# A graph-layer kernel on one core: adj as the weights of the last two row tiles, a bias spread by a matmul, weights on a block diagonal

## Chip, core and metric

One Trainium2 chip, one of its cores. The metric is the device time of one execution in microseconds (us); lower is better. Before the change it is 250.76 us, the median of 3 runs (250.6 to 250.86).

## What is computed

N = 5000 nodes, 64 features, all float32; `adj` is 5000 x 5000 and dense in memory (100 MB).

```python
h = jnp.maximum(_layernorm(x, axis=-1), 0.0)
neighbors = adj @ h
neighbors = neighbors / (num_neighbors[:, None] + 1e-7)
out = jnp.concatenate([h, neighbors], axis=-1) @ fc_w.T + fc_b
return x + jax.nn.relu(out)
```

The kernel multiplies first by the right half of `fc_w` (g = h @ W2.T) and then by `adj`, so that for every node out = x + relu(h @ W1.T + b + (adj @ g) / count).

## The kernel before

`adj` comes transposed, in three column groups of 2048, 2560 and 392 columns (GROUPS, WIDTH). Its 5000 rows are cut into 39 tiles of 128 (CH = 39), and 8 rows are left over (REM). A tile of `raw` holds 128 rows (the contraction) of a group's columns (output nodes). `multiply` (L574) has the 64 columns of g of that tile as stationary weights and streams the adj columns past them. The sums stand in the PSUM tensors acc0 to acc5 with features on the lanes; acc5 is the tensor `turned`, which takes the last 392 columns in two sides of SIDE = 196. A float32 matmul runs as two instructions, each with its own load of weights, so one tile of the last group is 4 instructions.

The order of TensorE's work is written out by hand: over all loads in order, with the steps of the layer norm's transposes (`turn`, TURN_AFTER), the weighing (`weigh`, WEIGH_AFTER), the counts (`spread`), the 8 remaining rows (`remainder`) and the turning back of finished banks (`flip`, FLIP_AFTER) put in after named tiles. A group's sums go back to node-major by `scale` (DVE, with the reciprocal count), `flip` (PE transpose) and `finish` (DVE, relu and x).

The last 392 columns end the kernel. `preload_self` (L611) puts the self part of the 392 nodes into y0 and y1 as the start of a sum. After tile 38, `scale_last` (L474) multiplies the sums by the reciprocal counts into sums0, `flip_last` (L618) adds their transpose to y0 and y1, `finish_last` (L491) applies relu and adds x, and SP stores 98 KB (L243) and waits for it. The 392 nodes stand on 98 lanes (LAST_LANES), four to a lane.

The SP queue issues x (L236, L239) and then all 40 adj loads (`load`, L224). A load waits on `load_used` when its place in `raw` is still in use. The ACT queue issues the two copies of the weights and the bias (`load_weights`, L278), the counts, the 8 remaining rows of each group (`load_rem`, L264) and the stores of the first two groups. The 8 rows stand on lanes 0, 4, ..., 28 of `adj_rem` (REM_STEP = 4); its other lanes are zero, and so are those of `ht_rem`.

`weigh` takes two node tiles at a time, in the lane halves of `ht`. Each half has its own matmul with the copy of the weights in the same half of `w_both`: 64 lanes by 128 columns, self and neighbour part. `copy_g` (ACT) takes the neighbour part and `add_bias` (DVE) the self part plus the bias.

Of the kernel before, what the change touches and what calls it, by code (L numbers as in the profile page):

```python
# [12 lines left out]
LANES = 128  # L13
# [8 lines left out]
REM_STEP = 4  # L22
# [17 lines left out]
def gnn_layer(nc, x, adj_groups, num_neighbors, fc_t, fc_b, out):  # L40
# [69 lines left out]
    PRELOAD_AFTER = (2, 25)  # L110
    LN_OPS = 8

    with ExitStack() as ctx:
# [22 lines left out]
        w_both = sb("w_both", [2 * F, 2 * F])  # L136
# [3 lines left out]
        ones = sb("ones", [LANES, HALF])  # L140
# [3 lines left out]
        rstd = sb("rstd", [LANES, BT])  # L144
        warm = sb("warm", [LANES, 1])
# [10 lines left out]
        nn_loaded = sem("nn_loaded")  # L156
        weights_loaded = sem("weights_loaded")
        bias_loaded = sem("bias_loaded")
        landed = [sem(f"landed{k}") for k in range(LANDINGS)]
# [15 lines left out]
        self_copied = sem("self_copied")  # L175
        spread_done = sem("spread_done")
# [6 lines left out]
        out_ready = sem("out_ready")  # L183
        stored = sem("stored")
# [29 lines left out]

        def bcast(v):
            return v.unsqueeze(2).to_broadcast([LANES, v.shape[1], F])
# [6 lines left out]
        @block.sync  # L223
        def _(sp):  # L224
            def load(n):
                g, m, i0, i1 = LOADS[n]
                w = WIDTH[g]
                if loads_before(n):
                    sp.wait_ge(load_used, loads_before(n))
                r = RUN if m < FULL else TAIL_RUN  # L230
                rows = adj_groups[g][m * BLOCK:m * BLOCK + r * LANES, 0:w].rearrange("(p i) c -> p (i c)", i=r)
                sp.dma_start(raw[:, place(n):place_end(n)], rows[:, i0 * w:i1 * w]).then_inc(loaded(n)[0], 16)  # L232

            for k in range(2):
# [12 lines left out]
        def _(pool):  # L247
# [3 lines left out]
                                    pattern=[[-1, LANES]], channel_multiplier=1).then_inc(ident_ready, 1)  # L251
            nc.gpsimd.memset(adj_rem[:], 0.0).then_inc(rem_cleared, 1)
            nc.gpsimd.memset(ones[:], 1.0).then_inc(ones_ready, 1)
# [3 lines left out]
            pool.wait_ge(ones_ready, 2)  # L257
# [5 lines left out]
        def _(act):  # L263
            def load_rem(g):  # L264
                w = WIDTH[g]
                if g:
                    act.wait_ge(rem_used, g)
                else:
                    act.wait_ge(rem_cleared, 2)
                lanes = slice(0, REM * REM_STEP, REM_STEP)  # L270
                k = w // BLOCK
                if k:
                    act.dma_start(adj_rem[lanes, 0:k, 0:BLOCK],
                                  adj_groups[g][REM0:N, 0:w].rearrange("r (k c) -> r k c", k=k)).then_inc(rem_loaded, 16)
                else:
                    act.dma_start(adj_rem[lanes, 0, 0:w], adj_groups[g][REM0:N, 0:w]).then_inc(rem_loaded, 16)

            def load_weights():  # L278
                for s in range(2):
                    act.dma_start(w_both[s * F:(s + 1) * F, :].rearrange("r (k c) -> r k c", k=2),  # L280
                                  fc_t.rearrange("(k r) c -> r k c", k=2)).then_inc(weights_loaded, 16)
                act.dma_start(bias[:], fc_b.rearrange("(a f) -> a f", a=1).to_broadcast([LANES, F])
                              ).then_inc(bias_loaded, 16)
# [32 lines left out]
            def copy_g(b):  # L316
                act.wait_ge(weighed, b + 1)
                for s in range(2):
                    t0 = BT * b + RUN * s
                    nc.scalar.activation(g_sb[:, t0:t0 + RUN, :], split(y[s][:])[:, :, F:2 * F], ACT.Copy  # L320
                                         ).then_inc(g_copied, 1)
# [14 lines left out]
            load_weights()  # L336
# [17 lines left out]
            store(1)  # L354
            act.wait_ge(stored, 32)

        @block.vector
        def _(dve):
            nc.vector.memset(warm[:], 1.0).then_inc(warm_ready, 1)
            nc.vector.memset(x_sb[PAD0:LANES, ROWS:TILES, :], 0.0).then_inc(x_cleared, 1)  # L360
            nc.vector.memset(nn[:], 1.0).then_inc(nn_cleared, 1)
# [11 lines left out]
            def normalize(b):  # L373
                base = LN_OPS * b
                dve.wait_ge(x_loaded[0], 32)
                if b == SETS - 1:
                    dve.wait_ge(x_loaded[1], 16)
# [26 lines left out]
            def add_bias(b):  # L404
                if b == 0:
                    dve.wait_ge(bias_loaded, 16)
                for s in range(2):
                    m = 2 * b + s
                    to = blocks(out_sb, m, m + 1) if m < FULL else out_sb[:, ROWS:TILES, :]
                    dve.wait_ge(g_copied, 2 * b + s + 1)  # L410
                    nc.vector.tensor_tensor(to, split(y[s][:])[:, :, 0:F],  # L411
                                            bias[:].unsqueeze(1).to_broadcast([LANES, RUN, F]),
                                            ALU.add).then_inc(self_copied, 1)
# [60 lines left out]
            def scale_last(g):  # L474
                wait_sums(g, LAST)
                dve.wait_ge(flipped, LAST)
                for i in range(2):
                    nc.vector.tensor_tensor(sums[0][:, i * LAST_LANES:(i + 1) * LAST_LANES],  # L478
                                            tile_major(acc[LAST][:, 0:SIDE], 2)[:, i, :],
                                            rnn_bc[:, ALONE, BLOCK // 2 + i * LAST_LANES:BLOCK // 2 + (i + 1) * LAST_LANES],  # L480
                                            ALU.mult).then_inc(scaled, 1)
# [9 lines left out]
            def finish_last():  # L491

                for i in range(2):
                    dve.wait_ge(flipped, LAST + i + 1)
                    done = nc.vector.scalar_tensor_tensor(  # L495
                        tail_half(out_sb, i), y[i][0:LAST_LANES, 0:2 * F].rearrange("p (s f) -> p s f", s=2), 0.0,
                        tail_half(x_sb, i), ALU.max, ALU.add)
                done.then_inc(out_ready, 1)
# [12 lines left out]
            add_bias(4)  # L511
            for b in range(SETS):
# [9 lines left out]
            scale_last(G - 1)  # L522
# [3 lines left out]
        def _(pe):  # L526
# [9 lines left out]
            def weigh(b):  # L536

                pe.wait_ge(turned_copied, b + 1)
                if b:
                    pe.wait_ge(self_copied, 2 * b)  # L540
                for i in range(RUN):
                    for s in range(2):
                        k = slice(s * F, (s + 1) * F)
                        c = i * LANES
                        apart = b == SETS - 1 and s == 1
                        last = nc.tensor.matmul(y[s][:, c:c + (F if apart else 2 * F)], ht[b % 2][k, c:c + LANES],  # L546
                                                w_both[k, 0:F if apart else 2 * F], start=True, stop=True)
                        if apart:
                            h = ht_rows[k, i:REM0 - TAIL0:TAIL_RUN] if i < TAIL_RUN else ht_rem[k, :]
                            last = nc.tensor.matmul(y[s][:, c + F:c + 2 * F], h, w_both[k, F:2 * F],  # L550
                                                    start=True, stop=True)
# [22 lines left out]
            def multiply(n, i):  # L574
                g, m, i0, i1 = LOADS[n]
                t = m * RUN + i
                c = place(n) + (i - i0) * WIDTH[g]
                for b in banks(g):
                    for s, c0, width in sides(g, b):
                        last = nc.tensor.matmul(acc[b][s * HALF:(s + 1) * HALF, 0:width], g_sb[:, t, :],  # L580
                                                raw[:, c + c0:c + c0 + width], start=t == 0, stop=t == CH - 1,
# [4 lines left out]
            def remainder(g):  # L586
                pe.wait_ge(rem_loaded, 16 * (g + 1))
                for b in banks(g):
                    for s, c0, width in sides(g, b):
                        c = c0 % BLOCK  # L590
                        last = nc.tensor.matmul(acc[b][s * HALF:(s + 1) * HALF, 0:width], g_sb[:, CH, :],  # L591
                                                adj_rem[:, c0 // BLOCK, c:c + width], start=False, stop=False,
                                                tile_position=(0, s * HALF))
# [17 lines left out]
            def preload_self():  # L611

                pe.wait_ge(out_ready, LAST)
                for i in range(2):
# [3 lines left out]
            def flip_last():  # L618
                for i in range(2):
                    pe.wait_ge(scaled, LAST + i + 1)  # L620
                    nc.tensor.matmul(y[i][0:LAST_LANES, 0:2 * F], sums[0][:, i * LAST_LANES:(i + 1) * LAST_LANES],  # L621
                                     ident[:], start=False, stop=True).then_inc(flipped, 1)

            pe.wait_ge(ident_ready, 1)
# [3 lines left out]
            for n in range(len(LOADS)):  # L628
                g, m, i0, i1 = LOADS[n]
                pe.wait_ge(*loaded(n))  # L630
                for i in range(i0, i1):
# [8 lines left out]
                    if at == SPREAD_AFTER:  # L640
                        pe.wait_ge(ones_ready, 4)
# [8 lines left out]
            flip_last()  # L650
# [27 lines left out]
```

## Time and profile before

| what | value |
|---|---|
| median of 3 runs | 250.76 us (250.6 to 250.86) |
| the profiled execution | 251.19 us, its span 249.4 us |
| PE / PEld / DVE / ACT / POOL busy | 200.8 / 82.7 / 40.3 / 15.2 / 3.6 us |
| DMA | 102.84 MB in 8424 packets, 412 GB/s over the span |
| granted TensorE clock, mean | 0.972 of full |

The profiled execution's own time is 1.8 us above its span, and 0.4 us above the median. PE is the matmul stream, PEld the loading of weights that runs beside it; DVE, ACT and POOL are the vector, scalar and GpSimd engines; SPq and ACTq are the DMA issues on those queues. Times in the views are microseconds from the start of the span; a group of instructions that is merged into one row has its first start and the length it covers.

### The profile page before, as it was taken

Reading aid. Unit: us, or ns where it says so; the run is one execution under the profiler, and the core shown is the slowest. Engines: PE = TensorE matmul, PEld = TensorE weight load, DVE = VectorE, ACT = ScalarE, POOL = GpSimd, SP = SyncE. Lnnn points to the kernel's source line nnn. Section 1 sums busy time; section 2 is a strip of 40 time slices with the busy share of each in tenths; the row PEclk is TensorE's granted clock in tenths of the full one; section 3 lists DMA queues with packets and bytes.
Section 4 is the critical chain, followed back from the end, with each engine's and each line's share of the span. In section 5 each row is a group of like instructions: output and inputs, shape, how many; then the busy total and the mean of one; then the engine's idle time right before and its main releaser. Section 6 shows DMA issues by size and latency. Waiting matters only on the chain.

```text
span 249.4 us, 2504 instructions
## 1 busy us (share of the span) xinstructions
PE 200.8 (80%) x1122; PEld 82.7 (33%) x1122; DVE 40.3 (16%) x89; ACT 15.2 (6%) x35; POOL 3.6 (1%) x12
## 2 busy tenths in 40 slices
PE   0159887796796995998996299997398998798994
PEld 0133232332332531332342034332132433235782
DVE  0740543321100050006102001000000000003411
ACT  2130220120110010004000000000000000000000
POOL 5000000000000000000000000000000000000000
PEclk9999999999999999999999779999779999999999
DMA  9899999999999999999999999999999999999991
GB/s 294 376 387 426 421 425 426 457 438 415 428 431 426 431 428 432 451 420 407 427 462 440 427 427 400 427 467 431 434 427 400 430 430 426 419 413 418 416 388 64
DMA packets 8424, 102.84 MB, mean 412 GB/s; under 512 B 1542, under 2 KB 3350, under 8 KB 5086
## 3 DMA queue, kind: packets, MB, share of 16 engines
q1 hardware_dynamic: 6468, 101.22, 95.7%
q10 hardware_dynamic: 1946, 1.46, 1.8%
q8 instruction: 9, 0.15, 0.2%
q14 instruction: 1, 0.01, 0.0%
HBM read 101.40 MB, written 1.28 MB: 412 GB/s over the span
## 4 chain that ended last, share of the span: by engine, by line
DMA 70%; PE 27%; SPq 1%; DVE 0%; issue 0%
DMA raw<-adj_group 70%; PE acc L580 24%; PE acc L591 2%; PE turned L580 1%; SPq L236 0%; SPq L232 0%; PE y L605 0%; DVE out_sb L495 0%; PE y L621 0%; SPq L239 0%; PE turned L591 0%; DVE sums L478 0%
## 5 line engine op out<-in xcount | busy, mean ns | idle before, releaser
L580 PE MATMUL acc<-raw,g_sb 128*64 128x512 f32 (+1 forms) x780 | 162.4, 572 | 30.7 <-DMA raw<-adj_group 30.7
L580 PEld LDWEIGHTS acc<-raw,g_sb 128*64 128x64 f32 x780 | 56.1, 142 | 129.7 <-issue 88.1
L580 PE MATMUL turned<-raw,g_sb 128*64 128x196 f32 x156 | 14.9, 334 | 1.0 <-DMA raw<-adj_group 1.0
L461 DVE TENSOR_TENSOR sums<-acc,rnn_bc 128x512 f32<-128x512 f32 x4 | 2.6, 686 | 78.7 <-PE acc L580 76.7
L533 PE MATMUL turned<-ident,h_pairs 128*128 128x128 f32 x20 | 3.7, 315 | 11.6 <-DVE h_pairs L402 11.6
L580 PEld LDWEIGHTS turned<-raw,g_sb 128*64 128x64 f32 x156 | 10.5, 136 | 4.2 <-DMA raw<-adj_group 2.2
L411 DVE TENSOR_TENSOR out_sb<-y,bias 128x256 f32<-128x256 f32 x10 | 3.8, 420 | 43.9 <-ACT g_sb L320 35.5
L546 PE MATMUL y<-w_both,ht 64*128 64x128 f32 (+1 forms) x80 | 7.6, 317 | 1.6 <-DMA w_both<-fc_t 1.6
L487 DVE TENSOR_TENSOR out_sb<-y,out_sb 128x512 f32<-128x512 f32 (+1 forms) x5 | 3.2, 639 | 33.4 <-PE y L605 32.3
L432 DVE TENSOR_TENSOR rnn_diag<-ident,rnn 128x512 f32<-128x512 f32 x8 | 5.0, 685 | 21.4 <-PE y L570 21.4
L546 PEld LDWEIGHTS y<-w_both,ht 64*128 64x128 f32 x80 | 6.2, 215 | 5.2 <-issue 3.2
L533 PEld LDWEIGHTS turned<-ident,h_pairs 128*128 128x128 f32 x20 | 2.4, 156 | 14.8 <-issue 14.0
L320 ACT ACTIVATE g_sb<-y 128x256 f32<-128x256 f32 x10 | 3.3, 381 | 36.9 <-PE y L546 23.3
L570 PE MATMUL y<-rnn_diag,ones 128*64 128x512 f32 (+1 forms) x20 | 4.6, 552 | 0.8 <-ACT rnn_bc L326 0.7
L390 DVE TENSOR_REDUCE var<-sums 128x8 f32<-128x512 f32 x5 | 3.4, 686 | 10.6 <-ACT sums L294 10.6
L326 ACT ACTIVATE rnn_bc<-y 128x512 f32<-128x512 f32 (+1 forms) x5 | 2.9, 587 | 26.8 <-PE y L570 26.8
L379 DVE TENSOR_REDUCE mean<-x_sb 128x8 f32<-128x512 f32 (+1 forms) x6 | 3.5, 590 | 5.2 <-DMA x_sb<-x 5.2
L314 ACT ACTIVATE ht<-turned 128x512 f32<-128x512 f32 x5 | 3.0, 597 | 21.0 <-PE turned L533 21.0
L591 PE MATMUL acc<-adj_rem,g_sb 128*64 128x512 f32 (+1 forms) x20 | 4.2, 550 | 0.0
L294 ACT ACTIVATE sums<-cen 128x512 f32<-128x512 f32 x5 | 3.1, 627 | 7.3 <-DVE cen L386 6.0
L386 DVE TENSOR_TENSOR cen<-x_sb,mean 128x512 f32<-128x512 f32 (+1 forms) x6 | 3.5, 603 | 0.2
L398 DVE TENSOR_TENSOR cen<-cen,rstd 128x512 f32<-128x512 f32 x5 | 3.5, 692 | 0.2
(51 smaller groups left out, 36.4 us busy)
## 6 DMA issues: line engine op xcount, KB each, us to landing
raw<-adj_group SPq DMA_DIRECT2D x9, 4096.0 KB, 31.8
raw<-adj_group SPq DMA_DIRECT2D x5, 5120.0 KB, 27.0
raw<-adj_group SPq DMA_DIRECT2D x8, 2560.0 KB, 28.3
raw<-adj_group SPq DMA_DIRECT2D x7, 784.0 KB, 25.8
raw<-adj_group SPq DMA_DIRECT2D x3, 1280.0 KB, 21.2
raw<-adj_group SPq DMA_DIRECT2D x1, 3072.0 KB, 28.5
raw<-adj_group SPq DMA_DIRECT2D x4, 392.0 KB, 19.1
x_sb<-x SPq DMA_DIRECT2D x2, 576.0 KB, 4.7
```

Of the source, the lines that this page charges most:

```text
L320: nc.scalar.activation(g_sb[:, t0:t0 + RUN, :], split(y[s][:])[:, :, F:2 * F], ACT.Copy).then_inc(g_copied, 1)
L379: last = nc.vector.tensor_reduce(narrow(mean[:]), rows, AX_X, ALU.add)
L386: last = nc.vector.tensor_tensor(wide(cen[:]), rows, m.unsqueeze(len(m.shape)).to_broadcast(list(rows.shape)), ALU.subtract)
L390: nc.vector.tensor_reduce(var[:], sums[0][:].rearrange("p (t f) -> p t f", f=F), AX_X, ALU.add).then_inc(ln_dve, 1)
L398: nc.vector.tensor_tensor(c, c, bcast(rstd[:]), ALU.mult).then_inc(ln_dve, 1)
L411: nc.vector.tensor_tensor(to, split(y[s][:])[:, :, 0:F], bias[:].unsqueeze(1).to_broadcast([LANES, RUN, F]), ALU.add).then_inc(self_copied, 1)
L432: last = nc.vector.tensor_tensor(split(to[:, s, :]), ident[:].unsqueeze(1).to_broadcast(shape), rnn[:, m + s:ROWS:FULL].unsqueeze(2).to_br ...
L533: last = nc.tensor.transpose(turned[:, c], h_pairs[b % 2][:, c], ident[:])
L546: last = nc.tensor.matmul(y[s][:, c:c + (F if apart else 2 * F)], ht[b % 2][k, c:c + LANES], w_both[k, 0:F if apart else 2 * F], start=Tru ...
L570: last = nc.tensor.matmul(y[b % 2][k, c], ones[:, 0:HALF], r, start=True, stop=True, tile_position=(0, s * HALF))
L580: last = nc.tensor.matmul(acc[b][s * HALF:(s + 1) * HALF, 0:width], g_sb[:, t, :], raw[:, c + c0:c + c0 + width], start=t == 0, stop=t == ...
L591: last = nc.tensor.matmul(acc[b][s * HALF:(s + 1) * HALF, 0:width], g_sb[:, CH, :], adj_rem[:, c0 // BLOCK, c:c + width], start=False, sto ...
```

## The change

- The last two tiles (37 and 38, DIRECT = 2) of the last group are multiplied the other way round (`multiply_direct`): adj is the stationary operand, 98 of its columns with a stride of two elements, and g streams past it. The result is node-major and is added straight into y0 and y1. The sums over tiles 0 to 36 are copied (`copy_last`) and turned (`flip_last`) between tile 37 and tile 38.
- Since y then holds undivided sums, the self part of the 392 nodes is multiplied by its count beforehand (`count_self`), and the division comes at the end: on ACT for y0 (relu with a scale), on DVE for y1.
- The bias is loaded as one row and spread to all lanes by a matmul with ones, into acc4 (`ALONE`), from where DVE copies it.
- `w_both` is a block diagonal, 128 lanes by 256 columns; `weigh` is one matmul for a pair of tiles. Its two blocks are loaded by SP ahead of the adj loads; ACT no longer loads weights.
- The 8 remaining rows stand on lanes 0, 16, ..., 112 of `adj_rem` and `ht_rem`, and the columns of an odd block are loaded as two halves, by a DMA of their own.
- The last part of x comes as 96 lanes on SP and 2 lanes on ACT.

```diff
-REM_STEP = 4
+REM_STEP = 16
...
+    DIRECT = 2
+    TURNED_LOADS = [(g, m * RUN + i1) for g, m, _, i1 in LOADS].index((G - 1, CH - DIRECT)) + 1
...
-            sp.wait_ge(x_cleared, 1)
-            sp.dma_start(tail(x_sb), tail_nodes(x)).then_inc(x_loaded[1], 16)
+            sp.dma_start(tail(x_sb)[0:PAD0], tail_nodes(x)[0:PAD0]).then_inc(x_loaded[1], 16)
+            sp.wait_ge(weights_cleared, 1)
+            for s in range(2):
+                k = slice(s * F, (s + 1) * F)
+                sp.dma_start(w_both[k, s, :].rearrange("r (k c) -> r k c", k=2), fc_t.rearrange("(k r) c -> r k c", k=2)
+                             ).then_inc(weights_loaded, 16)
...
-                act.dma_start(bias[:], fc_b.rearrange("(a f) -> a f", a=1).to_broadcast([LANES, F])
-                              ).then_inc(bias_loaded, 16)
+                act.dma_start(bias_row[0:1, :], fc_b.rearrange("(a f) -> a f", a=1)).then_inc(bias_loaded, 16)
+                act.wait_ge(x_cleared, 1)
+                act.dma_start(tail(x_sb)[PAD0:LAST_LANES], tail_nodes(x)[PAD0:LAST_LANES]).then_inc(x_loaded[1], 16)
...
+            nc.scalar.activation(std[:, 0:1], warm[:], ACT.Relu)
+
+            act.wait_ge(added_up, 1)
+            for k in range(2):
+                done = nc.scalar.activation(last_relu[0:LAST_LANES, k * F:(k + 1) * F], y[0][0:LAST_LANES, k * F:(k + 1) * F],
+                                            ACT.Relu, scale=rnn[0:LAST_LANES, ROWS + 2 * k:ROWS + 2 * k + 1])
+            done.then_inc(last_divided, 1)
...
-            def scale_last(g):
-                wait_sums(g, LAST)
+            def count_self():
+
+                dve.wait_ge(self_copied, 2 * SETS)
+                nc.vector.tensor_tensor(out_sb[:, ROWS:TILES, :], out_sb[:, ROWS:TILES, :], bcast(nn[:, ROWS:TILES]),
+                                        ALU.mult).then_inc(self_counted, 1)
+
+            def copy_last():
+                dve.wait_ge(load_used, TURNED_LOADS)
                 dve.wait_ge(flipped, LAST)
                 for i in range(2):
-                    nc.vector.tensor_tensor(sums[0][:, i * LAST_LANES:(i + 1) * LAST_LANES],
...
+                    nc.vector.tensor_copy(sums[0][:, i * LAST_LANES:(i + 1) * LAST_LANES],
+                                          tile_major(acc[LAST][:, 0:SIDE], 2)[:, i, :]).then_inc(scaled, 1)
...
+                dve.wait_ge(added_up, 2)
+                o = tail_half(out_sb, 1)
+                nc.vector.tensor_tensor(o, y[1][0:LAST_LANES, 0:2 * F].rearrange("p (s f) -> p s f", s=2),
+                                        rnn[0:LAST_LANES, ROWS + 1:TILES:2].unsqueeze(2).to_broadcast([LAST_LANES, 2, F]),
+                                        ALU.mult).then_inc(summed, 1)
+                dve.wait_ge(summed, LAST + 1)
+                nc.vector.scalar_tensor_tensor(o, o, 0.0, tail_half(x_sb, 1), ALU.max, ALU.add)
+                dve.wait_ge(last_divided, 1)
+                nc.vector.tensor_tensor(tail_half(out_sb, 0), last_relu[0:LAST_LANES, :].rearrange("p (s f) -> p s f", s=2),
+                                        tail_half(x_sb, 0), ALU.add).then_inc(out_ready, 1)
...
+            def multiply_direct(n, i):
+                g, m, i0, _ = LOADS[n]
+                t = m * RUN + i
+                c = place(n) + (i - i0) * WIDTH[g]
+                for k in range(2):
+                    for s in range(2):
+                        last = nc.tensor.matmul(y[k][0:LAST_LANES, s * F:(s + 1) * F],
+                                                raw[:, c + s * SIDE + k:c + (s + 1) * SIDE:2], g_sb[:, t, :],
+                                                start=False, stop=t == CH - 1 and s == 1)
+                    if t == CH - 1:
+                        last.then_inc(added_up, 1)
...
+                    if g == G - 1 and at[1] >= CH - DIRECT:
+                        multiply_direct(n, i)
+                        if at[1] == CH - 2:
+                            flip_last()
+                        continue
...
-            flip_last()
```

The order of TensorE's work at the end of the program, before; `turned` is the sum of the last 392 columns, `landed13`, `landed14` and `landed15` are the arrivals of tiles 36, 37 and 38:

```order
L580 MATMUL turned<-raw,g_sb 64x196 x3
L580 MATMUL turned<-raw,g_sb 64x196 [waits landed13]
L580 MATMUL turned<-raw,g_sb 64x196
L580 MATMUL turned<-raw,g_sb 64x196 [waits landed14]
L580 MATMUL turned<-raw,g_sb 64x196
L580 MATMUL turned<-raw,g_sb 64x196 [waits landed15]
L580 MATMUL turned<-raw,g_sb 64x196
L621 MATMUL y<-ident,sums 98x128 [waits scaled] x2
```

and with the change:

```order
L636 MATMUL turned<-raw,g_sb 64x196 x3
L636 MATMUL turned<-raw,g_sb 64x196 [waits landed13]
L636 MATMUL turned<-raw,g_sb 64x196
L688 MATMUL y<-g_sb,raw 98x64 [waits landed14]
L688 MATMUL y<-g_sb,raw 98x64 x3
L679 MATMUL y<-ident,sums 98x128 [waits scaled] x2
L688 MATMUL y<-g_sb,raw 98x64 [waits landed15]
L688 MATMUL y<-g_sb,raw 98x64 x3
```

The two matmuls that turn the sums now stand ahead of the last tile, and each of the last two tiles has four matmuls of 64 streamed columns in place of two of 196.

The start of SP's queue, before:

```order
L236 DMA x_sb<-x 128x1152 x2
L239 DMA x_sb<-x 98x2x128 [waits x_cleared]
L232 DMA raw<-adj_group 128x8192 x4
L232 DMA raw<-adj_group 128x8192 [waits load_used] x5
L232 DMA raw<-adj_group 128x6144 [waits load_used]
```

and with the change:

```order
L261 DMA x_sb<-x 128x1152 x2
L266 DMA x_sb<-x 96x2x128
L270 DMA w_both<-fc_t 64x2x64 [waits weights_cleared]
L270 DMA w_both<-fc_t 64x2x64
L257 DMA raw<-adj_group 128x8192 x4
L257 DMA raw<-adj_group 128x8192 [waits load_used] x5
```

The two loads of weights come ahead of the first adj load on this queue, and SP waits there for a clearing of `w_both` in place of one of `x_sb`.

## Rows read from the trace of the kernel before

**Rows 1.** The page: busy time by engine, DMA queues, and one group (busy us, mean ns).
```profile
PE 200.8 (80%) x1122; PEld 82.7 (33%) x1122; DVE 40.3 (16%) x89; ACT 15.2 (6%) x35; POOL 3.6 (1%) x12
...
q1 hardware_dynamic: 6468, 101.22, 95.7%
q10 hardware_dynamic: 1946, 1.46, 1.8%
...
L546 PE MATMUL y<-w_both,ht 64*128 64x128 f32 (+1 forms) x80 | 7.6, 317 | 1.6 <-DMA w_both<-fc_t 1.6
```

**Rows 2.** Windows: stretch, length, busy time of PE, PEld, DVE, ACT, POOL, clock, DMA share, GB/s.
```profile
2.50:5.50 3.00, 0.00 (x0) 0.00 (x0) 0.00 (x0) 0.00 (x0) 1.84 (x6) 1.00 0.96 376
2.50:12.00 9.50, 0.39 (x2) 0.42 (x3) 4.26 (x9) 0.84 (x2) 1.84 (x6) 1.00 1.05 410
20.00:100.00 80.00, 66.73 (x353) 24.72 (x351) 18.43 (x44) 7.95 (x21) 0.00 (x0) 1.00 1.00 429
100.00:220.00 120.00, 103.26 (x528) 38.80 (x526) 7.46 (x12) 2.94 (x5) 0.00 (x0) 0.94 1.00 429
```

**Rows 3.** The chain of waits that ended last, by line.
```profile
by line: DMA raw<-adj_group 70.5%; PE acc L580 23.8%; PE acc L591 1.5%; PE turned L580 1.0%; SPq L236 0.3%; issue 0.3%; SPq L232 0.3%; PE y L605 0.2%; DVE out_sb L495 0.2%; PE y L621 0.2%; SPq L239 0.2%; PE turned L591 0.1%; DVE sums L478 0
```

**Rows 4.** Timeline of the end, all engines: start, length, what.
```profile
235.83 1.10 PE L607 MATMUL y<-ident_twice,cen 128*128 128x64 f32 x8
...
240.28 3.87 PE L580 MATMUL turned<-raw,g_sb 128*64 128x196 f32 x44
...
244.33 0.55 PE L580 MATMUL turned<-raw,g_sb 128*64 128x196 f32 x4 [0.18 <-DMA raw<-adj_group]
...
245.27 0.55 PE L580 MATMUL turned<-raw,g_sb 128*64 128x196 f32 x4 [0.39 <-DMA raw<-adj_group]
245.87 0.43 DVE L478 TENSOR_TENSOR sums<-turned,rnn_bc 128x98 f32<-128x98 f32 x2 [8.01 <-PE turned L580]
...
246.18 0.68 PE L621 MATMUL y<-ident,sums 128*98 128x128 f32 x4 [0.36 <-DVE sums L478]
246.68 0.51 DVE L495 SCALAR_TENSOR_TENSOR out_sb<-y,x_sb 98x128 f32<-98x128 f32 x2 [0.39 <-PE y L621]
247.22 0.36 SPq L243 DMA_DIRECT2D out<-out_sb  x1
```

**Rows 5.** Windows of the end.
```profile
229.00:239.00 10.00, 9.59 (x100) 7.27 (x100) 4.15 (x8) 0.00 (x0) 0.00 (x0) 1.00 1.02 413
239.00:242.50 3.50, 3.50 (x42) 2.74 (x40) 0.00 (x0) 0.00 (x0) 0.00 (x0) 1.00 1.03 392
242.50:244.00 1.50, 1.50 (x20) 1.14 (x16) 0.00 (x0) 0.00 (x0) 0.00 (x0) 1.00 0.80 296
244.00:245.50 1.50, 0.93 (x10) 0.40 (x8) 0.00 (x0) 0.00 (x0) 0.00 (x0) 1.00 0.17 57
```

**Rows 6.** DMA issues: what, queue, count, KB each, median us to landing.
```profile
x_sb<-x SPq DMA_DIRECT2D x2, 576.0 KB, 4.7
...
x_sb<-x SPq DMA_DIRECT2D x1, 98.0 KB
...
adj_rem<-adj_group ACTq DMA_DIRECT2D x1, 80.0 KB
w_both<-fc_t ACTq DMA_DIRECT2D x2, 32.0 KB, 9.2
adj_rem<-adj_group ACTq DMA_DIRECT2D x1, 64.0 KB
bias<-fc_b ACTq DMA_DIRECT2D x1, 32.0 KB, 22.4
...
adj_rem<-adj_group ACTq DMA_DIRECT2D x1, 12.2 KB
```

**Rows 7.** Timeline of the start.
```profile
0.75 0.85 SPq L236 DMA_DIRECT2D x_sb<-x  x2
...
0.91 1.42 ACTq L280 DMA_DIRECT2D w_both<-fc_t  x2
...
0.98 0.27 DVE L360 MEMSET x_sb<- 32x256 f32 x1
...
1.65 0.46 SPq L239 DMA_DIRECT2D x_sb<-x  x1
...
2.16 24.33 SPq L232 DMA_DIRECT2D raw<-adj_group  x5
...
11.62 1.09 PE L533 MATMUL turned<-ident,h_pairs 128*128 128x128 f32 x4 [11.62 <-DVE h_pairs L402]
...
17.48 8.64 PE L580 MATMUL acc<-raw,g_sb 128*64 128x512 f32 x32 [1.11 <-DMA raw<-adj_group]
```

**Rows 8.** Single lines L607, L550, L546, L621: instructions, ns min/median/max, first and last start.
```profile
L607 PE MATMUL y<-ident_twice,cen x8: 275/275/323, 235.8 to 236.7; 128*128 128x64 f32 x8
L550 PEld LDWEIGHTS y<-w_both,ht_rows x6: 248/254/260, 85.2 to 86.5; 64*128 64x128 f32 x6
L546 PEld LDWEIGHTS y<-w_both,ht x80: 182/188/330, 14.3 to 86.8; 64*128 64x128 f32 x80
L621 PEld LDWEIGHTS y<-ident,sums x4: 161/164/165, 246.2 to 246.5; 128*98 128x98 f32 x4
```

More of the change, by code:

```diff
@@ L110, in gnn_layer @@
     PRELOAD_AFTER = (2, 25)
+    DIRECT = 2
+    TURNED_LOADS = [(g, m * RUN + i1) for g, m, _, i1 in LOADS].index((G - 1, CH - DIRECT)) + 1
     LN_OPS = 8
+    REM_LOADS = [sum(1 + (w > BLOCK and w % (2 * BLOCK) > 0) for w in WIDTH[:g + 1]) for g in range(G)]
     with ExitStack() as ctx:
@@ L232, in load, with load_x @@
                 sp.dma_start(raw[:, place(n):place_end(n)], rows[:, i0 * w:i1 * w]).then_inc(loaded(n)[0], 16)
-            for k in range(2):
+            def load_x(k):
                 r = slice(ROWS // 2 * k, ROWS // 2 * (k + 1))
@@ L317, in copy_g @@
                 act.wait_ge(weighed, b + 1)
[L318 to L321, printed above, removed]
+                to = g_sb[:, BT * b:BT * (b + 1), :].rearrange("p (s i) f -> p i s f", s=2)
+                for k in range(2):
+                    nc.scalar.activation(to[:, 2 * k:2 * k + 2, :, :], weighed_parts(k, 1), ACT.Copy).then_inc(g_copied, 1)
             def copy_spread(b):
@@ L405, in add_bias @@
                 if b == 0:
[L406 to L413, printed above, removed]
+                    dve.wait_ge(bias_spread, 1)
+                    nc.vector.tensor_copy(bias[:], acc[ALONE][:, 0:F]).then_inc(bias_copied, 1)
+                    dve.wait_ge(bias_copied, 1)
+                for k in range(2):
+                    dve.wait_ge(g_copied, 2 * b + k + 1)
+                    for s in range(2):
+                        m = 2 * b + s
+                        to = blocks(out_sb, m, m + 1) if m < FULL else out_sb[:, ROWS:TILES, :]
+                        last = nc.vector.tensor_tensor(to[:, 2 * k:2 * k + 2, :], weighed_parts(k, 0)[:, :, s, :],
+                                                       bias[:].unsqueeze(1).to_broadcast([LANES, 2, F]), ALU.add)
+                    last.then_inc(self_copied, 1)
             def invert_neighbors():
@@ L511, in _ @@
             add_bias(4)
+            count_self()
             for b in range(SETS):
@@ L540, in weigh @@
                     pe.wait_ge(self_copied, 2 * b)
+                apart = b == SETS - 1
+                w = 3 * F if apart else 4 * F
                 for i in range(RUN):
[L542 to L551, printed above, removed]
+                    c = i * LANES
+                    last = nc.tensor.matmul(weighed_tiles(i)[:, 0:w], ht[b % 2][:, c:c + LANES], flat(w_both[:])[:, 0:w],
+                                            start=True, stop=True)
+                    if apart:
+                        h = ht_rows[F:LANES, i:REM0 - TAIL0:TAIL_RUN] if i < TAIL_RUN else ht_rem[F:LANES, :]
+                        last = nc.tensor.matmul(weighed_tiles(i)[:, w:4 * F], h, w_both[F:LANES, 1, F:2 * F],
+                                                start=True, stop=True)
                 last.then_inc(weighed, 1)
@@ L577, in multiply @@
                 c = place(n) + (i - i0) * WIDTH[g]
+                end = CH - 1 if g < G - 1 else CH - DIRECT - 1
                 for b in banks(g):
```

85 lines of the change are left out of this document (53 added, 32 removed).

## The prediction

> **What bounds the kernel now.** I read the chain of waits first. It gives 70.5% of the span to the adj loads, and its remaining PE pieces are the places where the chain passes through a multiplication that frees room for a load [rows 3]. PE is busy for 80% of the span and every other engine for less [rows 1], so the reader should look next at whether the DMA engines ever rest. They do not: from 20 to 220 us the DMA share is 1.00 at 429 GB/s, in windows in which PE has idle time to spare [rows 2]. The load queue carries 101.22 MB, and its packets take 95.7% of 16 engines' span [rows 1]. PE work in the body can therefore be added or removed without a change of the time; what counts is the start of the stream of loads, the work the DMA engines have in it, and what follows its last byte.
>
> The start is tight. Transfers reach 376 GB/s from 2.5 us, and the mean from 2.5 to 12 us is 410 GB/s [rows 2], though the first adj load is issued only at 2.16 us [rows 7], behind 1250 KB of x [rows 6]. There is no hole between x and adj.
>
> At the end the last load but one lands just ahead of 244.33 us and the last just ahead of 245.27 us; PE waits for both [rows 4]. Then follows a chain of 2.0 us up to the issue of the store at 247.22: multiplication of tile 38 (0.55 us), scaling, turning, relu and addition of x [rows 4]. The store and its landing take the last 2.2 us of the span. The DMA share falls from 1.03 to 0.80 between 242.5 and 244 and to 0.17 after it [rows 5], so the DMA engines do not end together.
>
> **The change part by part, start.** The two loads of weights move from ACT's queue to SP's, ahead of the first adj load. On ACT the two issues take 1.42 us [rows 7]; on SP they push the first adj issue from 2.16 to about 3.6 us. The bytes are the same. From both sides: nothing, if the engines still have x before them when adj's descriptors come; 1.4 us, if the stream of loads starts that much later. x and the weights are 1314 KB [rows 6], 1.35 MB, which at 424 GB/s (101.22 MB in 95.7% of the span [rows 1]) occupy the engines for 3.2 us, from 2.5 to 5.7. The first x load was issued at 0.75 us and data flows at about 2.5 us, 1.75 us later; an adj load issued at 3.6 would flow at 5.35 us. I take **0**, because the margin is 0.35 us and positive. The wait that SP gets, for the clearing of `w_both`, is over by then: the clearing of x_sb ends at 1.25 us [rows 7] and the new clearing follows it, while SP comes to the wait at 2.1 us.
>
> The bias was 128 pieces of 256 B and is now one. 32 KB at 429 GB/s are 0.08 us, the lower bound. The small transfers' queue took 1.8% of 16 x 249.4 us for 1946 packets [rows 1], 37 ns each; 8 such packets on each of 16 engines are 0.30 us, the upper bound. Those packets have 750 B on average, so a packet of 256 B is nearer to the lower bound: **-0.15 us** (0.08 to 0.30) in the work of every DMA engine, and so in all later landings. The bias landed 22.4 us after its issue [rows 6], which held the DVE; now one packet and a matmul replace it. It has to be there for the first transposes, at 11.62 us [rows 7]. The first multiplication of adj starts at 17.48 us with four loads of 4096 KB issued (39 us of transfers at 429 GB/s), so a start some microseconds later would cost nothing either.
>
> The block diagonal halves the number of weighing matmuls; four narrower additions per pair of tiles replace two; the count multiplication is one more DVE instruction near 88 us. All of it lies under the loads: from 20 to 100 us PE is idle for 13 of 80 us and DVE for 61 [rows 2]. **0**. If that cover were gone, the weighing would give back at most half of the 7.6 us of L546 [rows 1], and the ten added DVE additions and the count would cost some 0.2 us each.
>
> The 8 remaining rows keep their 156 KB [rows 6]; only their lanes change, and 512 columns of the second group come in a second small DMA. **0** in the forecast; the alternative is a rival.
>
> **The change at the end.** What is removed behind the last landing: scaling, turning and relu, from the end of tile 38's matmuls at 245.82 to 247.19. What comes: tile 38 as 8 instruction pairs (4 matmuls, two instructions each), and on DVE a multiplication, a relu with addition, and one more addition. ACT does its half beside it.
>
> Price of a pair with 64 streamed columns: L607 has it, with 128 weight columns; eight take 1.10 us [rows 4] and one 0.28 [rows 8], that is (1.10 - 0.28) / 7 = 0.117 us from start to start. The lower bound is the present tile, 44 instructions in 3.87 us, 0.088 us each [rows 4]. The new one has 98 weight columns; 98/128 of 0.117 is **0.09 us**, near that lower bound. The upper bound has the stride in it: with weights read with a stride of three elements the weight load took 254 ns at L550, against 188 without at L546 [rows 8]. 66 ns more make 0.16 us.
>
> With 0.09: tile 37 occupies PE from 244.33 to 245.05. Meanwhile DVE copies the sums of tiles 0 to 36, complete at 244.15 [rows 4], in the 0.43 us of L478, so `flip_last` needs no wait; four instructions of about 0.1 us end at 245.45. Tile 38 has landed by then and waits 0.2 us for PE. It ends at 245.45 + 7 x 0.09 + 0.28 = 246.36. DVE then takes 0.04 + 0.29 (as L495) + 0.04 + 0.26 (as L478) + 0.22 = 0.85 us and ends at 247.21, against 247.19 now. **0**, between -0.05 (with 0.088, everything shifted) and, with 0.16, tile 37 until 245.61, the turning until 246.01, tile 38 until 247.4 and DVE until 248.3, +1.1. So the early turning does leave the path, but what is late next is PE itself.
>
> On the stride a page bears: the Trainium skill, SBUF — State Buffer, "Door 1: The DMA port swizzle", says that reads run at full rate when at least two hits fall into a 16-byte line, which a stride of two float32 still has and a stride of three has not. L550 against L546 agrees for three [rows 8]; no row shows two. By that rule the sum at the end would be the 0 taken above, otherwise up to +1.1.
>
> **Sum:** -0.15 + 0 + 0 = -0.15 us. Against the profiled execution that is 251.19 - 0.15 = 251.04; the median of the runs shown lies 0.43 below it, so 250.76 - 0.15 = **250.6 us**. A measurement of this kernel tells about 0.2% (0.5 us) from no change, so this counts as the same.
>
> **Rival A, faster: the DMA engines end closer together.** From 242.5 to 245.5 they moved 1.5 x 296 + 1.5 x 57 = 530 KB [rows 5]; at 392 GB/s, 1.35 us, they would have ended at 243.85 and not at 245.25. So up to 1.4 us lie in their inequality. The remaining rows are 156 KB [rows 6]; if eight engines take them, each has 19.5 KB more than the others, 0.74 us at 26.5 GB/s. If 16 lanes of distance, or the evenly divisible 96 lanes of x, spreads that, the late engines gain up to 0.74 us: with three quarters of it 250.6 - 0.55 = 250.05, between 249.9 and 250.3. For it: the fall of the DMA share. Against it: no row shows which engine is late, and eight rows stay eight rows. The Trainium skill, DMA: Bandwidth & Descriptors, "Why a DMA increments its semaphore by 16 and not by 1", says that the number of engines is the largest divisor up to 16 of the outer count, 8 at both distances; no row of this trace shows that split. By it this rival would get nothing from the spacing.
>
> **Rival B, slower: the strided weights cost what L550 shows.** The price is 66 ns for each of the 16 strided pairs of tiles 37 and 38; it shows in the verdict when a pair takes over 0.13 us (15 x 0.04 = 0.6 us, less the 0.15 of the bias). At 0.16 it is 250.76 - 0.15 + 1.1 = 251.7. For it speaks the only strided weight load in the trace; against it the smaller stride.
>
> **Rival C, slower: adj starts late.** If the weights' small pieces hold SP's queue for the whole 1.4 us: 250.76 + 1.4 - 0.15 = 252.0. Against it: the margin above. Half of it would give 251.3.
>
> **Rival D, slower: the remaining rows fall on four engines.** If the lane chooses the engine, lanes 0, 16, ..., 112 can share engines in pairs; four engines then have 39 KB more, 0.74 us above now: 250.6 + 0.74 = 251.35, if one of these is among the last. The Trainium skill's page on DMA, "The descriptor swizzle", has such a mapping for a transfer to 128 lanes, by which these eight lanes make four engines; no row shows it.
>
> **The numbers.** Forecast 0.56 (own range 250.2 to 251.1), A 0.27, B 0.08, C 0.05, D 0.04. Faster by over 0.2%: A, and 0.06 of the forecast's own spread, 0.33. Slower: most of B and C and three quarters of D, 0.15. Same: 0.52. The range 250.0 to 251.4 leaves out B, half of C and a quarter to a third of A, about 0.2.
>
> **What would show it.** Right: the window 2.5 to 12 us again near 410 GB/s although the first adj issue is at 3.4 to 3.7 us; PE without a pause from tile 37 to the end of tile 38, with tile 38 waiting 0.1 to 0.3 us for it; the last matmul at 246.2 to 246.4 and the store's issue at about 247.1 us. Wrong at the start: GB/s of that window below 390. Wrong on the stride: weight loads of the direct matmuls over 210 ns, where L621's shape has 164. Wrong on the engines: the last adj landing moves by more than 0.3 us from 245.2, with a different fall of the DMA share after 242.5. The weights should land before 10 us, and DVE no longer wait for the bias.

## The result, and the profile after

The changed kernel takes 251.31 us (251.16 to 251.75, 10 runs), the kernel before 250.85 us on the same chip (250.6 to 251.09, 10 runs): 0.17% slower, ratio 1.0017, 95% interval 1.0009 to 1.0024. Forecast were 250.6 us and a gain of 0.15. In a later set of runs it came out the same, 251.51 against 251.03, ratio 1.0016 (1.0008 to 1.0025). One execution of h1 below took 258.57 us at a granted clock of 0.869; its nine others have a median of 250.28 us, and the 250.35 given for it counts all ten.

The profiled execution alone would mislead. The profiled run of before (251.19 us, span 249.4) lies above all ten of its timed runs, whose median is 250.85. That of the change (251.25 us, span 249.3) is an ordinary one. So the two profiles show nearly equal spans, and the loss has to be found in rates and by variants, not by subtracting two spans.

Page of the kernel after, busy time and DMA queues (answers to [rows 1]):
```profile
PE 207.4 (83%) x1092; PEld 87.3 (35%) x1092; DVE 42.0 (17%) x103; ACT 15.9 (6%) x38; POOL 3.7 (1%) x13
...
q1 hardware_dynamic: 6754, 101.29, 96.1%
q10 hardware_dynamic: 1546, 1.36, 1.6%
```
PE does 6.6 us more: the 40 weighing matmuls of the block diagonal take 12.1 us, where the 80 before took 7.6 [rows 1]. 128 small packets are gone from the ACT queue and the weights' packets have moved over to SP's.

Windows of the kernel after: stretch, length, busy PE, PEld, DVE, ACT, POOL, clock, DMA share, GB/s (answers to [rows 2, 5]):
```profile
2.50:12.00 9.50, 1.28 (x5) 1.12 (x6) 4.43 (x10) 0.84 (x2) 1.99 (x5) 1.00 1.04 408
20.00:100.00 80.00, 71.84 (x320) 27.23 (x318) 17.16 (x48) 7.94 (x21) 0.00 (x0) 0.98 1.00 426
100.00:220.00 120.00, 102.86 (x526) 38.59 (x524) 7.46 (x12) 2.94 (x5) 0.00 (x0) 0.93 1.00 427
...
242.50:244.00 1.50, 1.27 (x16) 0.79 (x12) 0.18 (x2) 0.00 (x0) 0.00 (x0) 1.00 0.85 314
```
The start is as forecast: 408 GB/s against 410 [rows 2], though the first adj load is issued at 3.49 us. From 12 to 20 us the change is even ahead, 459 GB/s against 396; that is 504 KB or 1.2 us of transfers. But the body has lost 2 to 3 GB/s of 429 [rows 2]; over 200 us at 429 that is 2.5 x 200 / 429 = 1.2 us, and the lead is gone. The DMA share there is 1.00 as before: the engines are as busy and move less.

Timeline of the end of the kernel after (answers to [rows 4]):
```profile
239.90 3.87 PE L636 MATMUL turned<-raw,g_sb 128*64 128x196 f32 x44
243.82 0.43 DVE L530 COPY sums<-turned 128x98 f32<-128x98 f32 x2 [6.34 <-PE turned L636]
...
244.08 0.94 PE L688 MATMUL y<-g_sb,raw 128*98 128x64 f32 x8 [0.31 <-DMA raw<-adj_group]
...
244.86 0.63 PE L679 MATMUL y<-ident,sums 128*98 128x128 f32 x4
...
245.33 0.86 PE L688 MATMUL y<-g_sb,raw 128*98 128x64 f32 x8
...
246.22 0.29 DVE L545 TENSOR_TENSOR out_sb<-y,rnn 98x128 f32<-98x128 f32 x1 [1.98 <-PE y L688]
246.55 0.29 DVE L549 SCALAR_TENSOR_TENSOR out_sb<-out_sb,x_sb 98x128 f32<-98x128 f32 x1
246.76 0.28 DVE L551 TENSOR_TENSOR out_sb<-last_relu,x_sb 98x128 f32<-98x128 f32 x1
247.07 0.40 SPq L275 DMA_DIRECT2D out<-out_sb  x1
```
PE runs without a pause from tile 37 on, and tile 38 waits for PE, not for its landing: its row names no wait. From the start of tile 37 to the store's issue it is 247.07 - 244.08 = 2.99 us; before it was 247.22 - 244.33 = 2.89 [rows 4].

### The profile page after: what moved, and what is told of

It reads as the page before. It is cut to its first block, busy times and chain, and to the rows that moved or that the text cites. A ratio compares the mean times of both kernels' runs of the same rounds, so it can differ in the third digit from the quotient of the medians.

```text
span 249.3 us, 2467 instructions
## 1 busy us (share of the span) xinstructions
PE 207.4 (83%) x1092; PEld 87.3 (35%) x1092; DVE 42.0 (17%) x103; ACT 15.9 (6%) x38; POOL 3.7 (1%) x13
## 4 chain that ended last, share of the span: by engine, by line
DMA 67%; PE 28%; DVE 2%; ACT 1%; issue 1%; SPq 0%; DVEq 0%
DMA raw<-adj_group 65%; PE acc L636 23%; DMA x_sb<-x 2%; PE acc L649 2%; PE y L600 2%; PE y L688 1%; PE turned L588 0%; SPq L257 0%; DVE cen L429 0%; DVE cen L441 0%; DVE var L433 0%; DVE mean L422 0%; ACT g_sb L355 0%; ACT sums L329 0%; ACT ht L349 0%
## 5 line engine op out<-in xcount | busy, mean ns | idle before, releaser
L636 PE MATMUL turned<-raw,g_sb 128*64 128x196 f32 x148 | 13.7, 333 | 0.4 <-DMA raw<-adj_group 0.4
L600 PE MATMUL y<-w_both,ht 128*128 128x256 f32 (+1 forms) x40 | 12.1, 440 | 0.8 <-ACT ht L349 0.8
L457 DVE TENSOR_TENSOR out_sb<-y,bias 128x128 f32<-128x128 f32 x20 | 4.4, 284 | 37.9 <-ACT g_sb L355 37.9
L600 PEld LDWEIGHTS y<-w_both,ht 128*128 128x128 f32 x40 | 8.0, 217 | 5.6 <-issue 4.4
L699 PE MATMUL acc<-bias_row,ones 128*128 128x64 f32 x2 | 0.7, 450 | 6.4 <-DMA bias_row<-fc_b 6.4
```

The costliest lines, as they stand in the source:

```text
L457: last = nc.vector.tensor_tensor(to[:, 2 * k:2 * k + 2, :], weighed_parts(k, 0)[:, :, s, :], bias[:].unsqueeze(1).to_broadcast([LANES, 2, ...
L600: last = nc.tensor.matmul(weighed_tiles(i)[:, 0:w], ht[b % 2][:, c:c + LANES], flat(w_both[:])[:, 0:w], start=True, stop=True)
```

## The experiments

All times below are medians, each with the kernel before on the same chip (250.99 to 251.07). Variants of different sets are compared through it.

**Halves of the change.** e1 keeps the new end and the block diagonal and undoes the rest, the rows' distance with it; e2 undoes the end alone; e3 keeps only the block diagonal (and the odd block's remaining rows in halves, 4 lanes apart); e4 is the change with one number back:

```diff
-REM_STEP = 16
+REM_STEP = 4
```

> The change with its start undone: bias by a broadcast DMA, weights on ACT's queue ahead of it, x's tail as one DMA of 98 lanes, remaining rows 4 lanes apart; the turned-round last two tiles and the block diagonal stay. Theory 1 (the loss of 0.46 us is at the end of the program): as slow as the changed kernel, about 251.3, and span 249.3 or more. Theory 2 (the loss is at the start: adj is issued 1.33 us later behind the weights): back at 250.85 or below, 250.7 if the end gains the 0.15 us that the profile of the change shows.

> The change with its end undone: all 39 tiles multiplied with g as weights, scaling and turning after the last tile, no ACT work at the end. Theory 1 (loss at the end): 250.85 minus the bias's 0.15, about 250.7. Theory 2 (loss at the start): 251.3 or slightly more, 251.45.

> Only the block diagonal of the weights (and the halves of the odd block's remaining rows) on the kernel before; all DMAs of the start as before but for the layout of w_both, the end as before. Both theories: 250.85, since PE has idle time in the body. If the PE work of the weighing (12.1 us busy in place of 7.6) delays the first uses of the ring, up to 251.2.

> The change with the remaining rows 4 lanes apart again. Theory of the record (eight rows on eight DMA engines at both distances): the same as the change, 251.3. If the lanes of the rows matter to which engine ends last: 0.3 us or more away from it, on either side.

Measured: e1 250.79 (ratio 0.9989, 0.9978 to 0.9999), e2 250.99 (0.9995, 0.9987 to 1.0003), e3 251.29 (1.001, 0.9998 to 1.0021), e4 250.51 us (0.9979, 0.9971 to 0.9988). Neither theory holds: undoing the start and undoing the end both help. The answer is in e4: with its rows 4 lanes apart the change is 0.5 us faster than before, not slower. e1 and e3 have that distance too, so e1 does not tell the start from the rows.

**The distance of the remaining rows.** f1 changes only that number in the kernel before; f2 and f3 use 12 and 8 in the change; f4 is the change again.

> The kernel before with one number changed: the remaining rows 16 lanes apart in place of 4. Theory P (rows 16 apart slow every adj transfer while they are written): 0.6 to 0.9 us slower than before, and 118 to 128 us at about 417 GB/s in place of 444. Rival Q (the distance costs only together with the rest of the change): within 0.2 us of before, 118 to 128 us near 444 GB/s.

> The changed kernel with the rows 12 lanes apart (0, 12, ..., 84). The Trainium skill, SBUF — State Buffer, Door 1: The DMA port swizzle, has a map of lanes to ports by which these eight lanes lie on eight different ports, as lanes 4 apart do, while lanes 16 apart share four. Theory P1 (rows sharing a port collide): as fast as 4 apart, about 250.5, 118 to 128 us near 444 GB/s. Rival P2 (a row written outside its DMA engine's own lanes costs, shared or not; or distance itself costs): as the change, about 251.3, and near 417 GB/s.

> The changed kernel with the rows 8 lanes apart (0, 8, ..., 56): by the same map two rows on each of four ports, as with 16. P1: slow as the change, 251.2 to 251.4. P2 with distance: between 250.5 and 251.3. If the total of the shared rows did not matter at all: 250.5.

> The changed kernel once more, beside its variants on the same chip. If its loss holds here: 0.3 to 0.6 us above before, 0.7 to 0.9 above the same kernel with rows 4 apart (250.5).

| distance | kernel | us | ratio to before (95%) | GB/s, 118 to 128 us |
|---|---|---|---|---|
| 4 | before | 251.03 | 1 | 444 |
| 16 | before (f1) | 252.14 | 1.0045 (1.0033 to 1.0058) | 419 |
| 4 | change (e4) | 250.51 | 0.9979 (0.9971 to 0.9988) | 444 |
| 12 | change (f2) | 250.94 | 1.0000 (0.9991 to 1.0009) | 444 |
| 8 | change (f3) | 251.40 | 1.0011 (1.0002 to 1.0020) | 407 |
| 16 | change (f4) | 251.51 | 1.0016 (1.0008 to 1.0025) | 424 |

The second group's remaining rows are issued between 115.9 and 119.7 us in all of these, and are written in the stretch after it. The window of that stretch, of e4, f2, f3 and the change in that order:
```profile
118.00:128.00 10.00, 10.00 (x56) 3.88 (x54) 0.00 (x0) 0.00 (x0) 0.00 (x0) 1.00 1.05 444
```
```profile
118.00:128.00 10.00, 10.00 (x60) 4.07 (x58) 0.13 (x1) 0.00 (x0) 0.00 (x0) 1.00 1.07 444
```
```profile
118.00:128.00 10.00, 10.00 (x60) 4.10 (x58) 0.37 (x1) 0.00 (x0) 0.00 (x0) 1.00 1.03 407
```
```profile
118.00:128.00 10.00, 10.00 (x60) 4.07 (x58) 0.51 (x1) 0.00 (x0) 0.00 (x0) 1.00 1.04 417
```
27 GB/s less for 10 us are 270 KB, 0.63 us of transfers, around a DMA that carries 80 KB. But such a window hangs on its edges, since packets of 20 to 40 KB land in bursts: with f4 for the change it is 20 GB/s, and from 116 to 130 us e4 has 431, the change 424 and f4 428 GB/s.

Two measures of the traces do not depend on edges. The first is the mean duration of a single packet of the adj loads while the rows' 2 KB pieces are being moved: 32 KB packets around the first group's rows (between 55 and 64 us), 20 KB packets around the second group's (120 to 128 us). The second is the lag behind e4 in bytes moved since the start, divided by 427 GB/s, in us, averaged over three stretches: ahead of the first group's rows, between the two groups, and after the second.

| distance | run | 32 KB packet, ns | 20 KB packet, ns | lag, 34 to 52 us | 84 to 98 us | 142 to 220 us |
|---|---|---|---|---|---|---|
| 4 | e4 | 1218 | 767 | 0 | 0 | 0 |
| 4 | h4 | 1219 | 766 | -0.03 | 0.00 | -0.01 |
| 4 | before | 1227 | 769 | 0.92 | 0.84 | 0.80 |
| 16 | f1 | 1327 | 836 | 0.78 | 1.18 | 1.55 |
| 12 | f2 | 1262 | 822 | -0.01 | 0.24 | 0.50 |
| 8 | f3 | 1321 | 879 | -0.07 | 0.48 | 1.08 |
| 16 | f4 | 1287 | 863 | -0.07 | 0.30 | 0.83 |
| 16 | change | 1307 | 854 | 0.03 | 0.50 | 0.98 |

Between the groups, from 75 to 95 us, a 32 KB packet takes 1217 to 1220 ns in all of them. So the loss arises where the rows are written, about half at each group: 0.9 us in f4, 0.95 in the change, 1.2 in f3, and 0.9 in f1 against before (from 0.14 ahead of it to 0.75 behind). The medians differ by 1.0 (f4 against e4), 0.9 (f3) and 1.1 us (f1). And 12 apart is not free either: it loses 0.5 us at the same two places, its median 0.43 us; the window from 118 to 128 us did not show it. In the second group of f4 all 63 load packets take over 780 ns, in e4 none of 65: every engine's transfers slow down, not only those beside a row.

The rows themselves are moved as before. At each distance the first group's 32 pieces start in rounds of eight, one round per load packet (1.3 us apart in e4, 1.4 in the change), and are through in 4.5 to 6.5 us. That is eight engines with one row each; four engines with two rows each would need eight rounds.

What the rows have in common fits in part the map of lanes to ports in the Trainium skill, SBUF — State Buffer, "Door 1: The DMA port swizzle": by it eight rows lie on eight ports at distances 4 and 12, and on four at 8 and 16. The two shared cases are the slow ones, and distance alone does not order the times, since 12 is faster than 8. But 12 costs half as much without any shared port, so shared ports are not the whole cost. The rival of f2's expectation, that a row costs when it is written outside its own engine's lanes, would explain that half. No view here shows a port, and four shared ports do not say why all packets get longer: where the cost is is shown, what it is in the memory stays inferred.

**The end, one tile only, and the other parts.** All with rows 4 apart. g1 has `DIRECT = 1` and turns the sums after tile 38; g2 has the end as before; g3 loads the bias as before, by a DMA of 128 pieces; g4 has weights and x's last part on their old queues.

> Rows 4 apart, and only tile 38 with adj as the weights; the sums over tiles 0 to 37 are copied while PE works on tile 38 and turned after it. In the run with rows 4 apart tile 38 began 1.14 us after tile 37 (244.66 after 243.52) because the longer tile 37 and the turning stood in its way. Theory (PE is what ends last): 0.1 to 0.3 us faster than 250.5, that is about 250.3, the store's issue 0.2 us earlier. Rival (tile 38's landing ends last): no difference, 250.5.

> Rows 4 apart, everything else of the change but the end, which is as before. If the turned-round last tiles gain 0.2 to 0.3 us (as the change against its own version without them, 251.31 against 250.99, would even contradict): 250.7. If they gain nothing: 250.5. If they cost: below 250.5.

> Rows 4 apart, the bias again a DMA of 128 pieces of 256 B on ACT's queue. By the term of the prediction: 0.15 us (0.08 to 0.30) slower than 250.5, 250.65. Rival (nothing else of the change gains): all of the 0.5 us that rows 4 apart gain over before come from here, 251.0.

> Rows 4 apart, the weights on ACT's queue and the last part of x as one DMA of 98 lanes, as before; adj is issued 1.3 us earlier. By the prediction's term (0): 250.5. If the later issue of adj costs: 250.2 or below. If weights behind large adj packets or 98 lanes cost the DMA engines time: 250.7 or more.

Measured: g1 250.62 (0.9984, 0.9974 to 0.9994), g2 250.05 (0.9960, 0.9945 to 0.9975), g3 252.63 (1.0059, 1.0044 to 1.0075), g4 250.39 us (0.9986, 0.9966 to 1.0006). g1 gains nothing over e4: in its profile tile 38 now starts on its landing (244.74), but the turning then follows it and the store is issued at 247.03, 2.29 us later against 1.95 before [rows 4]. g2 says that the new end costs 0.46 us.

g4 against e4 (0.12) is inside its interval, but its executions do not lie together: nine take 250.27 to 250.74 us, three 251.79 to 252.47. The profiled one is the slowest. Its weights, issued on ACT's queue at 1.68 us, land 16.8 us later (4.6 on SP's in e4), the bias at 23.56, and the first multiplication of adj starts at 30.48 us against 17.99 in e4. PE is then busy without a pause from 54 to 100 us and still late, and between 100 and 118 us the loads fall to 385 GB/s (431 in e4): they wait for room in `raw`. The lag behind e4 is zero up to 98 us and 1.8 us from there on. In the kernel before, where the weights are issued at 0.91 us, they land after 9.2 us and PE starts at 17.48. So the queue of the weights does not move the median, and it decides how close PE comes to holding up the loads.

g3 is the surprise, 2.1 us for 128 small pieces. Its first microseconds, in windows:
```profile
2.50:3.50 1.00, 0.00 (x0) 0.00 (x0) 0.00 (x0) 0.00 (x0) 1.00 (x1) 1.00 0.80 263
3.50:4.50 1.00, 0.00 (x0) 0.00 (x0) 0.00 (x0) 0.00 (x0) 0.89 (x5) 1.00 0.61 235
4.50:5.50 1.00, 0.00 (x0) 0.00 (x0) 0.00 (x0) 0.00 (x0) 0.11 (x1) 1.00 0.33 112
...
2.50:12.00 9.50, 0.00 (x0) 0.00 (x0) 2.34 (x5) 0.63 (x1) 2.00 (x5) 1.00 0.90 327
```
and the same of e4, where the bias is one piece:
```profile
2.50:3.50 1.00, 0.00 (x0) 0.00 (x0) 0.00 (x0) 0.00 (x0) 1.00 (x1) 1.00 0.83 313
3.50:4.50 1.00, 0.00 (x0) 0.00 (x0) 0.00 (x0) 0.00 (x0) 0.89 (x5) 1.00 1.03 424
4.50:5.50 1.00, 0.00 (x0) 0.00 (x0) 0.00 (x0) 0.00 (x0) 0.10 (x1) 1.00 0.99 387
...
2.50:12.00 9.50, 1.16 (x5) 1.00 (x6) 4.32 (x9) 0.84 (x2) 1.99 (x5) 1.00 1.04 408
```
While the pieces are served the share of the DMA engines falls to a third. 81 GB/s less over 9.5 us are 770 KB, 1.8 us.

**The bias alone, its place, and the time outside the span.** h1 is the kernel before with the bias as one row; h2 is e4 with the broadcast, issued only after x has landed; h3 is the change with one memset more; h4 is g2 again.

```diff
             def load_weights():
+                act.wait_ge(bias_cleared, 1)
+                act.dma_start(bias_row[0:1, :], fc_b.rearrange("(a f) -> a f", a=1)).then_inc(bias_loaded, 16)
...
-                act.dma_start(bias[:], fc_b.rearrange("(a f) -> a f", a=1).to_broadcast([LANES, F])
-                              ).then_inc(bias_loaded, 16)
```

> The kernel before with one edit: the bias as one row (issued ahead of the weights on ACT's queue) and spread by a matmul; rows 4 lanes apart, end and weights as before. If the bias's 128 reads of one row cost the stream of loads more than the 0.15 us of the prediction, as the 2.1 us of the version with the broadcast at the start suggest: 0.35 us or more faster than before, 250.5 to 250.7. If only their early place in that version cost: 0.15 us or less.

> The changed kernel with rows 4 apart and the bias as 128 pieces again, but issued only once x has landed. Theory (the pieces hold up x and the start of adj because they come first and all read one row of HBM): most of the 2.1 us come back, 250.5 to 250.9, and the stretch 2.5 to 12 us is near 405 GB/s and not 327. Rival (the pieces cost 2 us wherever they are): 252.6.

> The changed kernel with one more memset of a 128x1 tile on POOL, which nothing uses. Between time and span lie 1.81 us in before and 2.0 us in the change and some variants, without a pattern in what they do. If that depends on the length or placement of the program: it may fall to 1.8, time 251.3 less 0.2. If it is a property of the change's work: stays at 2.0.

> Rows 4 apart and the end as before, the rest of the change kept, once more for a closer interval: 250.05, 0.8 to 1.0 us faster than before.

Measured: h1 250.35 (0.9974, 0.9965 to 0.9983), h2 251.17 (1.0008, 0.9999 to 1.0017), h3 251.23 (1.0007, 0.9999 to 1.0016), h4 250.04 us (0.9959, 0.9946 to 0.9972). The bias's single row is worth 0.64 us in the kernel before and 0.66 in the change (h2 against e4); issued at the very start, beside x, its broadcast costs 1.5 us more. In before and h2 the loss is spread over the stretch in which the pieces are moved, 9.8 to 19.3 us in h2. The window from 12 to 20 us of h2, where the pieces are in flight, and of e4:
```profile
12.00:20.00 8.00, 6.38 (x17) 3.48 (x17) 2.97 (x7) 1.98 (x5) 0.00 (x0) 1.00 0.98 397
```
```profile
12.00:20.00 8.00, 6.38 (x21) 3.67 (x22) 5.42 (x15) 1.98 (x5) 0.00 (x0) 1.00 1.06 455
```
By the lag in bytes h2 is 0.70 us behind e4 from 20 us on, and before 0.95. A piece of the bias itself takes 15 to 18 ns; the 32 KB load packets beside them take 1276 ns, in h2 as in before, and 1217 in e4. The weights are twice as many pieces of the same 256 B. In g4 they go over the same queue beside the loads, from 5.5 to 22 us, and the window has 454 GB/s and no lag (h1's profile shows 0.2 us). So number and size of the pieces are not what costs; that all of the bias's pieces read one row is the difference that is left, and it was not tested by itself.

h3 changes nothing: the time outside the span (device time less span, mean over each kernel's runs) stays at 1.99. It was 1.80 in before, 1.79 to 1.84 in e1, e2, f1, g2, g4, h1 and h4, and 1.99 to 2.07 in the change, e3, e4, f2, f3, g1, g3 and h2. I found no rule in that; 0.2 us of the change's loss lie there and stay open.

## Why the prediction was wrong

- **"The 8 remaining rows ... 0 in the forecast."** This is the step that turned the sign. The term was put at nothing because the bytes stay the same. Those 156 KB in other lanes cost 1.0 us (f4 against e4) and 1.1 us (f1 against before). Rival D gave the lanes a cost near that (0.74 us above) and a chance of 0.04, but by another way, four DMA engines with two rows each; the pieces start in rounds of eight, so that did not happen, and that its price is near is luck. What shows is that all load packets take longer while the rows are written (863 ns in place of 767 for 20 KB), at full DMA share. The rival looked at who carries the rows, and not at where they are written. The measured 251.31 us lies inside the stated range of 250.0 to 251.4, but it got there by this loss, with the sign against the forecast.
- **The bias, -0.15 (0.08 to 0.30).** It measured -0.64 (h1, interval -0.43 to -0.88), outside both bounds. The sum priced only the pieces' own time on the engines, and there it was right: 8 pieces on an engine at 18 ns are 0.14 us. What it left out is what they do to the load packets beside them (1276 ns in place of 1217). A wait was in plain view, 22.4 us to landing [rows 6], and was read only as a wait of DVE.
- **The end, 0 (-0.05 to +1.1).** The chain was right almost to the instruction: tile 37 was to take 0.72 us and took 0.78, tile 38 was to end 2.03 us after tile 37's start and ended after 2.11 (246.19), and DVE was to take 0.85 us and took 0.85. The stride of two costs next to nothing, as the rule of the Trainium skill's page SBUF — State Buffer, cited there, has it; the single line of the direct matmuls shows 169 ns a load, with L621's 164 [rows 8]:
```profile
L688 PEld LDWEIGHTS y<-g_sb,raw x16: 166/169/170, 244.1 to 245.9; 128*98 128x98 f32 x16
```
  Rival B falls with it. Yet the new end costs 0.46 us (e4 against g2 and h4), and 0.3 to 0.5 with the rows 16 apart (the change against e2). Of that 0.10 is in the chain: from tile 37's start to the store's issue it is 2.98 to 2.99 us in the change, e1, e4 and f4, and 2.86 to 2.90 in before, e2, e3, g2 and h4. 0.2 is outside the span, and the rest, some 0.15, these runs do not place. The forecast's 0 was near for the chain. With e1 against e3 the end even seems to gain 0.5 us; 0.26 of that is again outside the span, and both intervals are wide.
- **The start, 0.** Right: 408 GB/s from 2.5 to 12 us, adj issued at 3.49 us (forecast 3.6), weights 4.6 us to landing; g4's median gives 0.12 us, all of it outside the span. Rival C falls. That a later start of PE costs nothing holds for the most part: 11 to 12 us later it cost nothing in the profiles of e1 and e3 (28.8 us) and 1.8 us in that of g4 (30.5 us).
- **The block diagonal, 0.** Right for the span: 249.2 us in e3 as in before. Its 0.25 us of time are the 2.07 outside the span. The side remark that half of the weighing's 7.6 us could come back was wrong, since it rose to 12.1; PE had the room.
- **Rival A.** The engines' unequal ends did not become the gain; after the change the share still falls from 242.5 us on (0.85).

In a ladder, from measured kernels: before 251.0, with the bias once 250.35 (h1), with weights on SP, x in 96 lanes and the block diagonal 250.04 (h4), with the new end 250.51 (e4), with rows 16 apart 251.51 (f4). The change holds a gain of 0.95 us and gives it back, and more, with two of its own parts. The steps of 0.3 and 0.5 us come with intervals of about that size. h4, rows 4 apart and the old end, beats both kernels: 0.41% under before (0.28 to 0.54%).

## What to carry to other kernels

When the DMA engines are busy throughout, price a change of a small transfer by what it does to the large ones beside it: compare the bytes moved up to a time well before it and well after it, and the duration of single load packets beside it. Rows that look free to place are not: try the lanes of a small DMA as a parameter, and load a vector that all lanes need once and spread it on the chip. And when several edits come together, put each back alone; here the parts were worth about -0.6, -0.3, +0.5 and +1.0 us, and their sum told nothing of them.

## What the runs showed of the hardware

- Eight rows in 2 KB pieces, 64 and 80 KB, written 8 or 16 lanes apart make the 20 KB load packets beside them take 836 to 879 ns in place of 767, and the two groups cost 0.9 to 1.2 us together; 12 apart it is 822 ns and 0.5 us; 4 apart nothing shows.
- A DMA that reads one 256-byte row 128 times costs 0.65 us beside a stream of large loads, and 2.1 us when it is issued beside the first small loads, where the rate falls to 112 GB/s. 256 pieces of the same size from two loads of the weights cost nothing visible there (454 GB/s from 12 to 20 us in g4, 397 with the bias's pieces in h2).
- Two loads of 32 KB on ACT's queue land after 9.2 us when they are issued at 0.91 us (before), and after 16.8 to 17.2 us when they are issued at 1.68 us (e1, e3, g4).
- Weight loads of 98 float32 columns take 169 ns with a stride of two elements and 165 without (L688 and L679 of the change); with a stride of three they took 254 against 188 [rows 8].
- The time outside the span has two levels in kernels that differ little, 1.8 and 2.0 us.
